# Delta layer: order of the sync queue, of the gate and key transposes, and of the softmax

## The reference, cut to what matters

```python
q = _short_conv(hidden_states @ Wq.T, conv_q).reshape(b, l, H, DK)   # k and v_direct alike; H = 4, DK = 64
beta = jax.nn.sigmoid(hidden_states @ Wb.T)
delta_out = _delta_rule_chunkwise(q, k, v_direct, beta)              # chunks of 32 rows
#   q, k normalised; A = -(k*beta) @ k.T below the diagonal, M = 1 - A,
#   T = solve_triangular(M, eye); then a recurrence over the 16 chunks with T, q, k, v
local_s, local_m, local_l = (_fir(v_direct, f) for f in (fir_s, fir_m, fir_l))   # 3, 15, 63 taps
logits = jnp.einsum('bld,hpd->blhp', hidden_states, gate_w) + gate_b
probs = jax.nn.softmax(logits / temp, -1)
probs = probs * (1.0 - 5.0 * eps) + eps
o = probs[0]*local_s + probs[1]*local_m + probs[2]*local_l + probs[3]*delta_out + probs[4]*v_direct
return _rmsnorm(o, norm_w).reshape(b, l, H * DV) @ Wo.T
```

## Time and profile before

| | us |
|---|---|
| median of 3 runs (lowest, highest) | 4511.11 (4510.62, 4518.04) |
| the profiled execution | 4508.03 |
| its span, first to last instruction | 4506.2 |
| busy in the span: TensorE, VectorE, ScalarE, GpSimd | 3796.7, 2558.2, 1895.8, 1957.4 |
| first half's filters begin (TensorE, L5071) | 161.06 |
| second half's filters begin | 379.66 |

### The profile page before, as it was taken

How to read it: one execution, slowest core, us unless ns; L and a number is a source line. 1 busy time by engine, 2 the same in 40 slices (tenths; PEclk the granted TensorE clock), 3 DMA queues, 4 the chain that set the end, 5 groups by cost and what they waited for, 6 DMA issues and landing times. The chain is left out here.

```text
span 4506.2 us, 70923 instructions
## 1 busy us (share of the span) xinstructions
PE 3796.7 (84%) x26186; PEld 2609.8 (58%) x26186; DVE 2558.2 (57%) x4589; ACT 1895.8 (42%) x3440; POOL 1957.4 (43%) x2013
## 2 busy tenths in 40 slices
PE   7687787799999349949999799788888888999995
PEld 3647664467676149824544455466666666656663
DVE  6667453454554763357776322598888887312223
ACT  4142233333333112226666322588888886112222
POOL 6313462222322114432332111499999998332223
PEclk9798898899999669969999899899999999999997
DMA  5847542100000639844644200111111111822224
GB/s 195 253 133 239 143 106 72 66 10 10 20 10 10 215 92 291 233 149 120 174 131 125 84 33 24 54 52 52 51 50 50 42 47 62 268 88 47 46 45 133
DMA packets 327225, 453.44 MB, mean 101 GB/s; under 512 B 70470, under 2 KB 238902, under 8 KB 322758
## 3 DMA queue, kind: packets, MB, share of 16 engines
q1 hardware_dynamic: 304246, 418.03, 30.1%
q0 software_dynamic: 22512, 30.36, 3.7%
q10 hardware_dynamic: 128, 0.52, 0.0%
HBM read 308.29 MB, written 140.51 MB: 100 GB/s over the span
## 5 line engine op out<-in xcount | busy, mean ns | idle before, releaser
L3565 POOL TENSOR_TENSOR mamba_hC<-mamba_h_t,mamba_cb 128x512 f32<-128x512 f32 x512 | 671.5, 1339 | 80.1 <-DVE mamba_h_t L3078 76.6
L3078 DVE TENSOR_TENSOR_SCAN mamba_h_t<-mamba_dA,mamba_pB 128x512 f32<-128x512 f32 x512 | 596.2, 1206 | 116.2 <-PE mamba_pB L3456 51.8
L3456 PE MATMUL mamba_pB<-ident,mamba_dBT 128*128 128x128 f32 x2048 | 328.6, 285 | 61.3 <-DVE mamba_h_t L3078 55.4
L3254 ACT ACTIVATE mamba_dA<-mamba_delta,mamba_a_neg 128x512 f32<-128x512 f32 x512 | 356.5, 713 | 20.6 <-DVE mamba_h_t L3078 19.7
L3456 PEld LDWEIGHTS mamba_pB<-ident,mamba_dBT 128*128 128x128 f32 x2048 | 239.7, 144 | 198.9 <-issue 106.9
L3465 PE MATMUL mamba_pY<-ident,mamba_hC 128*128 128x128 f32 x2048 | 320.7, 281 | 17.6 <-POOL mamba_hC L3565 16.2
L1911 POOL TENSOR_SCALAR mqa_prob<-mqa_prob,mqa_rinv 128x128 f32<-128x128 f32 (+3 forms) x256 | 136.2, 532 | 425.5 <-DVE mqa_rinv L1687 424.6
L2350 DVE TENSOR_REDUCE mha_nmax<-mha_pM 128x1 f32<-128x384 f32 (+3 forms) x352 | 215.7, 635 | 105.5 <-PE mha_pM L2658 102.5
L3245 ACT ACTIVATE mamba_dBT<-mamba_eT,mamba_b_t 128x512 f32<-128x512 f32 x384 | 273.5, 713 | 0.1
L1501 POOL DMA_INDIRECT top_sum<-top_y,top_xg x71 | 110.2, 1552 | 352.3 <-ACT top_y L1290 341.8
L3465 PEld LDWEIGHTS mamba_pY<-ident,mamba_hC 128*128 128x128 f32 x2048 | 247.4, 145 | 26.9 <-POOL mamba_hC L3565 26.3
(11 more groups left out here) (627 smaller groups left out, 8791.6 us busy)
## 6 DMA issues: line engine op xcount, KB each, us to landing
expert_w<-in_L_ffn_W SPq DMA_DIRECT2D x48, 1024.0 KB, 6.1
delta_shared<-delta_w SPq DMA_DIRECT2D x64, 576.0 KB, 4.9
mamba_cb<-mamba_c SPq DMA_DIRECT2D x128, 256.0 KB, 3.1
mha_qkT<-mha_parts_d SPq DMA_DIRECT2D x96, 256.0 KB, 4.9
expert_w<-in_L_ffn_W SPq DMA_DIRECT2D x48, 256.0 KB, 9.0
top_w<-in_L_ffn_w SPq DMA_DIRECT2D x24, 512.0 KB, 10.3
delta_w<-delta_wst SPq DMA_DIRECT2D x17, 576.0 KB, 3.3
top_slots<-top_y SPq DMA_DIRECT2D x1, 9159.0 KB, 35.9
```

The source lines that it names most:

```text
L3078: nc.vector.tensor_tensor_scan(h_t[:, n % RH, :], dA[:, n % RA, :], pB[n % 2][:, :], 0.0, ALU.mult, ALU.add).then_inc(z["scan_ready"], 1)
L3254: nc.scalar.activation(dA[:, n % RA, :], delta[:, a % 2, ct, :], ACT.Exp, scale=a_neg[:, ct, s:s + 1])\
L3456: last = nc.tensor.transpose(pB[n % 2][:, tok(t)], dBT[:, r % RS, t, ct * P:(ct + 1) * P], c.ident[:, :])
L3565: nc.gpsimd.tensor_tensor(hC[:, n % RO, :], h_t[:, n % RH, :], cb[:, r % RC, :], ALU.mult)\
```

## The change

Four things, in both halves unless said otherwise.

1. SyncE's order, first half only. Ahead of the values it stores matrices 8 to 17 instead of 8 to 27; 18 to 21 go behind the values, 22, 23 and 24 behind the second, third and fourth group of Gram blocks, 25 and 26 behind beta, and 27 to 31 each behind one of the first five matrix loads. `vn` is loaded when the Gram stores and matrix 24's group are issued and its waits are met, as before.
2. TensorE turns the gate logits and lengths ahead of the keys, into banks 4 and 5 (it waits for `vr_ready` for that, no longer for all Gram copies).
3. ScalarE copies the keys instead of VectorE; between the second and the third of the eight copies it takes the gates' exponential. The root of the Gram diagonal moves behind `regroup(0)` and `regroup(1)`.
4. VectorE finishes the softmax, and clears the filters' pads, before it waits for `lt_in`.

```diff
@@ sync
                     if hf == 0:
-                        for g in range(8, FG - 4):
+                        for g in range(8, 18):
                             store_table(g)
                     sp.wait_ge(z["vr_ready"], NCH // 2 * (hf + 1))
...
+                    if hf == 0:
+                        for g in range(18, 22):
+                            store_table(g)
                     for i in range(NCH // 4):
...
+                        if hf == 0 and i >= 1:
+                            store_table(21 + i)
...
                     if hf == 0:
-                        for g in range(FG - 4, FG):
+                        for g in range(25, 27):
                             store_table(g)
...
                         sp.dma_start(wr[:, n % 3, :], w_d[g]).then_inc(w_ld[n % 3], 16)
+                        if hf == 0 and g + 27 < FG:
+                            store_table(g + 27)
@@ vector
-                    for i in range(NCH // 2):
-                        n = NCH // 2 * hf + i
-                        dve.wait_ge(z["kr_ps"], n + 1)
...
-                        nc.vector.tensor_copy(kr[:, 2 * i:2 * i + 2, :].rearrange("p n d -> p (n d)"), bank[6 + n % 2][:, :])\
-                            .then_inc(z["kr_ready"], 1)
                     for s in range(4):
                         dve.wait_ge(z["gl_ps"], 4 * hf + s + 1)
-                        ps, some = bank[2 + s % 2], slice(8 * (s % 2), 8 * (s % 2) + 8)
+                        ps, some = bank[4 + s % 2], slice(8 * (s % 2), 8 * (s % 2) + 8)
...
                     nc.vector.tensor_tensor(flat, flat, all_g(gred[:, :]), ALU.subtract).then_inc(z["soft_sub"], 1)
+                    dve.wait_ge(z["soft_exp"], hf + 1)
+                    link(nc.vector.tensor_reduce(gred[:, :], flat, AX.X, ALU.add))
+                    link(nc.vector.reciprocal(gred[:, :], gred[:, :]))
...
+                    nc.vector.tensor_tensor(rqk[:, 0, :, :], rqk[:, 0, :, :], gate[:, 1, :, :, 3], ALU.mult)\
+                        .then_inc(z["soft_done"], 1)
+                    dve.wait_ge(z["g_st"], 64 * NCH // 4 * (hf + 1))
+                    nc.vector.memset(vp[:, :, :, 0:PAD * HB], 0.0).then_inc(z["pads"], 1)
                     dve.wait_ge(z["lt_in"], 16 * (hf + 1))
@@ scalar
                     nc.scalar.activation(rqk[:, :, :, :], rqk[:, :, :, :], ACT.Sqrt).then_inc(z["root"], 1)
-                    act.wait_ge(z["lt_sum"], hf + 1)
-                    nc.scalar.activation(rs[:, :, :], rs[:, :, :], ACT.Sqrt).then_inc(z["lt_root"], 1)
-                    act.wait_ge(z["soft_sub"], hf + 1)
-                    nc.scalar.activation(gate[:, :, :, :, :], gate[:, :, :, :, :], ACT.Exp).then_inc(z["soft_exp"], 1)
+                    for i in range(NCH // 2):
+                        n = NCH // 2 * hf + i
+                        act.wait_ge(z["kr_ps"], n + 1)
+                        if n == NCH // 2:
+                            act.wait_ge(z["kr_kept"], 32)
+                        if i == NCH // 8:
+                            act.wait_ge(z["soft_sub"], hf + 1)
+                            nc.scalar.activation(gate[:, :, :, :, :], gate[:, :, :, :, :], ACT.Exp).then_inc(z["soft_exp"], 1)
+                        nc.scalar.activation(kr[:, 2 * i:2 * i + 2, :].rearrange("p n d -> p (n d)"), bank[6 + n % 2][:, :],
+                                             ACT.Copy).then_inc(z["kr_ready"], 1)
...
                     regroup(0)
                     regroup(1)
+                    act.wait_ge(z["lt_sum"], hf + 1)
+                    nc.scalar.activation(rs[:, :, :], rs[:, :, :], ACT.Sqrt).then_inc(z["lt_root"], 1)
                     filter_in(0)
@@ tensor
                     pe.wait_ge(z["logit_ready"], base + HB)
+                    pe.wait_ge(z["vr_ready"], NCH // 2 * (hf + 1))
+                    for s in range(4):
+                        if s >= 2:
+                            pe.wait_ge(z["gl_ready"], 4 * hf + s - 1)
+                        for i in range(8):
+                            t = 8 * (s % 2) + i
+                            if s < 2:
+                                last = nc.tensor.transpose(bank[4 + s % 2][:, i * GX:(i + 1) * GX],
...
                     for i in range(NCH // 2):
                         n = NCH // 2 * hf + i
...
                         last.then_inc(z["kr_ps"], 1)
-
-                    pe.wait_ge(z["g_ready"], NCH // 2 * (hf + 1))
-                    for s in range(4):
...
```

More of the change, by code:

```diff
@@ L4563, in _ @@
                     nc.vector.memset(xt[:, :, :, :], 0.0)
-                    for i in range(NCH // 2):
-                        n = NCH // 2 * hf + i
-                        dve.wait_ge(z["kr_ps"], n + 1)
-                        if n == NCH // 2:
-                            dve.wait_ge(z["kr_kept"], 32)
-                        nc.vector.tensor_copy(kr[:, 2 * i:2 * i + 2, :].rearrange("p n d -> p (n d)"), bank[6 + n % 2][:, :])\
-                            .then_inc(z["kr_ready"], 1)
                     for s in range(4):
                         dve.wait_ge(z["gl_ps"], 4 * hf + s + 1)
-                        ps, some = bank[2 + s % 2], slice(8 * (s % 2), 8 * (s % 2) + 8)
+                        ps, some = bank[4 + s % 2], slice(8 * (s % 2), 8 * (s % 2) + 8)
                         by_tile = ps[:, 0:8 * GX].rearrange("p (n x) -> p n x", x=GX)
@@ L4582, in _ @@
                             .then_inc(z["gl_ready"], 1)
-                    dve.wait_ge(z["g_st"], 64 * NCH // 4 * (hf + 1))
-                    nc.vector.memset(vp[:, :, :, 0:PAD * HB], 0.0).then_inc(z["pads"], 1)
                     for q in range(SQ):
@@ L4595, in _ @@
                     nc.vector.tensor_tensor(flat, flat, all_g(gred[:, :]), ALU.subtract).then_inc(z["soft_sub"], 1)
+                    dve.wait_ge(z["soft_exp"], hf + 1)
+                    link(nc.vector.tensor_reduce(gred[:, :], flat, AX.X, ALU.add))
+                    link(nc.vector.reciprocal(gred[:, :], gred[:, :]))
+                    link(nc.vector.tensor_tensor(flat, flat, all_g(gred[:, :]), ALU.mult))
+                    link(nc.vector.tensor_tensor(of_h, of_h, per_h(gscale[:, :]), ALU.mult))
+                    link(nc.vector.tensor_tensor(of_h, of_h, per_h(geps[:, :]), ALU.add))
+                    nc.vector.tensor_tensor(rqk[:, 0, :, :], rqk[:, 0, :, :], gate[:, 1, :, :, 3], ALU.mult)\
+                        .then_inc(z["soft_done"], 1)
+                    dve.wait_ge(z["g_st"], 64 * NCH // 4 * (hf + 1))
+                    nc.vector.memset(vp[:, :, :, 0:PAD * HB], 0.0).then_inc(z["pads"], 1)
                     dve.wait_ge(z["lt_in"], 16 * (hf + 1))
@@ L4607, in _ @@
                                                  ab[:, :, :].unsqueeze(2).to_broadcast([P, SQ, CH, CH]), ALU.mult))
[L4608 to L4615, removed]
                     def products(q):
@@ L5015, in _ @@
                     pe.wait_ge(z["logit_ready"], base + HB)
+                    pe.wait_ge(z["vr_ready"], NCH // 2 * (hf + 1))
[6 more added lines that the diff above has]
+                                last = nc.tensor.transpose(bank[4 + s % 2][:, i * GX:(i + 1) * GX],
+                                                           logit[0:GX, :, :, t].rearrange("p n b -> p (n b)"),
+                                                           c.ident[0:GX, 0:GX])
+                            else:
+                                nc.tensor.transpose(bank[4 + s % 2][:, i * GX:(i + 1) * GX], by_chunk[0:GX, t, :],
+                                                    c.ident[0:GX, 0:GX])
+                                last = nc.tensor.transpose(bank[4 + s % 2][:, 8 * GX + i * H:8 * GX + (i + 1) * H],
+                                                           by_chunk[SSK:SSK + H, t, :], c.ident[SSK:SSK + H, SSK:SSK + H])
+                        last.then_inc(z["gl_ps"], 1)
                     for i in range(NCH // 2):
```

## The result

The changed kernel takes 4525.84 us (median of 13 runs, 4510.67 to 4537.58) against 4514.06 (13 runs, 4506.73 to 4521.9) for the kernel before, run beside it: a ratio of 1.0023 [1.0012, 1.0033], slower by about 10 us. I had forecast 4507.5 and a range of 4499 to 4516. The profiled execution took 4519.42 us (span 4517.6), against 4508.03 (4506.2). Of the span's 11.4 us, 9.2 are there when the first half ends (TensorE's first turning of the next input, 259.29 against 250.13), and 10.6 at the first score of the layer's next part (474.16 against 463.61). What follows adds 0.9.

The account below looks back on a forecast made before the run. The prediction took each half's filter start and sixth matrix, then the ring of three loads, to set the pace. Gains of 2.5 and 1.1 us made 3.6: 4504.4 profiled, 4507.5 on the median's scale, range 4499 to 4516.

Parts of the forecast that it names:

- the 20.8: First half, SyncE's queue: predicted 20.8 us for values and Gram blocks before `vn`, apart from added stores and the last landing.
- The engines' moves: Gates, keys and softmax reordered: price nothing, up to 2 us if cover is gone; softmax gain 0, at most 1 a half.
- The last five stores now stand between the loads: First half, SyncE's loads: store 31 near 164.6, sixth load at 165.7, sixth matrix used at 174.2 against 176.71.
- a gain of 2.5: First half: sixth matrix in use at 174.2 instead of 176.71, a forecast gain of 2.5 us.
- rival C: First half's matrix loads starve behind stores waiting for builds and landings: 6.4 us slower, 4517.5; chance 0.15.
- the sum's own terms: Whole change: first half's gain of 2.5 us plus second half's 1.1 gives 3.6 us.
- the 7.5 us that the first load was to gain: First half: without stores 28 to 31 in SyncE's way, first matrix load issued at 148.8 instead of 156.28.
- The term of 1.1 us: Second half: filters start when the first matrix lands, 378.5 instead of 379.66, gaining 1.1 us (0 to 1.2).

Follow-up runs that it names:

- e1: Changed kernel with SyncE's old store order, keeping the moved TensorE, VectorE and ScalarE work: 4513.73 us, ratio 1.0002 [0.9988, 1.0017] to the kernel before.
- e7: Changed kernel, but GpSimd builds only the short filter's part of matrices 27 to 31, stores unchanged: 4516.95 us, ratio 1.0000 [0.9987, 1.0012] to the kernel before.
- e5: The kernel before, unchanged, run again for its trace on the same chip: 4515.86 us, ratio 1.0002 [0.9991, 1.0013].
- e8: Changed kernel with overwritten multiplications filling three of TensorE's first-half waits for a matrix: 4521.37 us, ratio 1.0011 [0.9999, 1.0023] to the kernel before.
- e11: Moved engines, stores 8 to 24 ahead of the values, each half's first three loads straight behind beta's stores: 4501.81 us, ratio 0.9985 to the kernel before.
- e6: The changed kernel, unchanged, run again beside the kernel before on one chip: 4524.59 us, ratio 1.0018 [1.0004, 1.0032].
- e9: The kernel before with only SyncE's order altered, storing matrices 8 to 24 ahead of the values: 4503.81 us, ratio 0.9983 [0.9970, 0.9996].
- e12: Changed kernel's moved engines with SyncE storing matrices 8 to 24 ahead of the values, a repeat run: 4506.64 us, ratio 0.9988 to the kernel before.

## Why the prediction was wrong

*What held.* Values at 106.9 (107.6 predicted), `vn` at 138.4 (137.6), the filters' start at 155.66 (155.5), the first load at 150.40 (148.8), GpSimd idle 20.77 us before matrix 23 (some 20), the second half's filters 1.1 closer to `vn`. Two of these came right in part by luck. From the values to `vn` the stores and the last landing added 10.7 us to the 20.8, not 9.3, while the values began 0.7 early. The first load was 1.6 late, and its matrix was in use 5.3 later instead of 6.7, so the start came out right. The engines' moves show no gain or loss (e1), as taken.

*The step that failed: "The last five stores now stand between the loads".* It forecast store 31 near 164.6, load 5 at 165.7 and the sixth matrix at 174.2. Measured: 171.0, 171.9 and 179.5. The 6.2 us of load 5 by the trace: store 25 landed near 152.1, not 150.6 (1.5); matrix 29 was ready 9.0 after 27, not 5.8, since 28 took 6.5 beside the scalings (3.2); 31 came 7.4 after 29, not 5.7, with a landing of 4.4 and a build of 3.0 (1.7); and 0.2 back. Then 7.6 from issue to use instead of 8.5: 5.3 late in all, and a gain of 2.5 had become a loss of 2.8. I had taken every build at the 2.46 of the earlier trace rows, where VectorE copied out of a bank or was idle. The earlier trace rows had the scalings' place right behind `bs`, and the change puts five builds exactly there; I had no term for what they do to a build.

*The mechanism was rival C's.* It was named with 0.15 and priced by store landings over 5.5 us. (By the sum's own terms the line was lower: the 2.5 us are gone at landings of 4.55, all 3.6 at 5.1.) The last five stores landed in 3.0 to 4.3 us. What made the loads starve was mostly the build in front of the store, not the landing behind it. In e7, without most of the building, 7.6 us of the 8.7 come back, and the sixth matrix is where the kernel before has it (176.31, e5 176.61). So the interleaving with short builds uses up the early start, and the builds make the loss. e7 takes away their ordinary length together with what VectorE adds, and doesn't divide the two. An estimate from the rows does: the scalings' 3.2 us in the chain, taken from 179.51, give 176.3, level with the 176.71 of before.

*What was counted as a gain.* Of the 7.5 us that the first load was to gain, my chain let 2.5 through to the sixth matrix. e8 shows that the filters' start has no weight: 5.9 us later and the same sixth matrix. The step from first load to sixth matrix is SyncE's, through the builds.

*Second half.* The term of 1.1 us failed too: it was there at the filters' start and gone at their end. From `vn` to the first score it takes 101.5 us, before 100.2. In the four traces with the old order of the engines it is 100.2 to 102.9, in those with the new one 101.1 to 103.3 (nine; e11, which alters this half's queue too, left out). Before, TensorE went from its turning straight into the first block, and the granted clock was 1.00 from 381.7 on; now it idles 3.62 ahead of that block, and the clock is 0.50 until 392.0 (11.03 us, before 8.90). That the clock is what took the 1.1 is argued from these rows; no run separates it.

*What stays open.* In e6 the loss grows from 5.9 us at the sixth matrix to 9.6 at the first score, in steps of 1.6 and 2.1 that are the size of the scatter between two traces of one kernel. A rival is not excluded for a part of it: from the sixth matrix to the half's end the four traces with the old order of the engines take 73.4 to 78.4 us, the ten with the new 76.6 to 80.9. The moved engines may cost some us there; e1's interval, and e9 against e12, are too wide to tell.

## What to carry to other kernels

A store that waits for its producer must not stand in front of a load in an in-order queue, unless the producer is known to be ahead: count the builds at the price they have beside whatever runs there then, not at the price of an idle stretch. Fill the queue's idle time instead: the SyncE order that stores 8 to 24 before it waits for the values gave 0.9983 to 0.9988 of the time, on either order of the engines. And a first transfer that starts earlier is worth only what the ones behind it gain.

## What was not expected of the hardware

A GpSimd build that meets a VectorE instruction with two operands in SBUF stands still while that runs: 2.62 us for 0.63, 6.2 to 6.5 for 2.46. VectorE pays less often but pays too: 3.26 for the second scaling instead of 2.29, 1.36 for a 128x224 product beside a build, where the one just ahead of it took 0.39 (164.65 and 164.22 in the changed kernel). In the changed kernel each wait of TensorE for a matrix of 3.6 us or more was followed by a block that began at a granted clock of 0.50 (155.66 to 160.0, 166.38 to 170.5, 179.51 to 185.0), and by e8 this cost nothing beyond the waits, because the matrices came no sooner.
